# A planned five-engine program: other durations in the table that lays down each engine's order, and another place for two powers of the keys

## The reference, cut to what matters

```python
x = x + tanh(g_xattn[0]) * mamba(ctx, layernorm(x))          # in_proj, conv4, silu, x_proj, softplus,
                                                              # scan over 512 positions for 512 channels x 16 states
x = x + tanh(g_ffn[0])   * out(silu(gate(n)) * val(n))        # n = layernorm(x); three BitLinear layers,
                                                              # weights rounded to -1, 0, 1, rows to 8 bits
x = x + tanh(g_xattn[1]) * (softmax(q_n k_n^T) v) @ Wo        # 16 heads of 128, q and k RMS-normalised, k and v from ctx
x = x + tanh(g_ffn[1])   * down(silu(gate) * up)              # four experts; row r goes to expert r % 4
```

## Time and profile before

| | us |
|---|---|
| three runs | 1846.49, 1849.45, 1853.75 (median 1849.45) |
| the profiled execution | 1849.74, its span 1847.9 |
| PE busy in the span | 1755.0 (95%) |
| DVE, ACT, POOL busy | 1301.5, 963.8, 681.7 |

### The profile page before, as it was taken

The page is one execution under the profiler, slowest core; times in us unless marked ns, Lnnn a source line. Parts: engine busy times, 40 slices in busy tenths (PEclk is TensorE's granted clock), DMA queues, the critical chain, the costliest instruction groups (busy, mean ns, idle before and its releaser), DMA issues.

```text
span 1847.9 us, 19510 instructions
## 1 busy us (share of the span) xinstructions
PE 1755.0 (95%) x6114; PEld 805.4 (44%) x6114; DVE 1301.5 (70%) x1899; ACT 963.8 (52%) x1919; POOL 681.7 (37%) x696
## 2 busy tenths in 40 slices
PE   8999899869998998999999999999999899999999
PEld 4333344324443444444444444444444344445543
DVE  4989786989999699899889898877532444412221
ACT  7989876447555546557466557554444334320100
POOL 2434422356463246457214456642123333300000
PEclk9999999989999999999999999999999999999999
DMA  7999823678851138887115779621122899837110
GB/s 262 244 293 291 259 100 109 188 186 198 207 145 37 52 82 210 222 208 196 57 36 114 178 188 249 159 58 57 46 69 80 235 285 292 237 100 273 40 51 28
DMA packets 159045, 292.11 MB, mean 158 GB/s; under 512 B 18424, under 2 KB 51704, under 8 KB 156000
## 3 DMA queue, kind: packets, MB, share of 16 engines
q1 hardware_dynamic: 141664, 227.95, 39.3%
q0 software_dynamic: 17280, 62.92, 17.6%
HBM read 169.51 MB, written 58.26 MB: 123 GB/s over the span
## 4 chain that ended last, share of the span: by engine, by line
PE 67%; DVE 15%; issue 6%; ACT 5%; DMA 5%; POOL 2%; SPq 1%; DVEq 0%; ACTq 0%; POOLq 0%
PE p L837 10%; PE p L814 8%; PE p L797 8%; PE p L848 7%; PE p L884 6%; PE p L692 5%; DVE s_M L1016 5%; PE p L771 4%; PE p L820 3%; PE p L899 3%; PE p L776 3%; PE p L741 2%; DVE s_M L1011 2%; DVE s_M L1023 2%; DVE s_U L1165 1%
## 5 line engine op out<-in xcount | busy, mean ns | idle before, releaser
L1016 DVE TENSOR_TENSOR_SCAN s_M<-s_M 128x1024 f32<-128x1024 f32 x128 | 297.3, 2323 | 12.5 <-ACT s_M L1277 10.0
L1165 DVE CUSTOM_DVE_ANT_0 s_U<-p,s_U 128x512 f32<-128x512 f32 x256 | 187.7, 745 | 167.0 <-PE p L814 164.7
L814 PE MATMUL p<-s_U 128*128 128x512 f32 x512 | 266.8, 609 | 4.5 <-DVE s_U L1165 3.4
L797 PE MATMUL p<-s_U 128*128 128x512 f32 x512 | 253.6, 604 | 5.1 <-DMA s_U<-in_Wq 2.4
L1517 POOL DMA_DIRECT2D s_u<-s_M x120 | 112.8, 941 | 358.1 <-DVE s_M L1023 323.7
L1558 POOL TENSOR_SCALAR s_U<-s_U 128x512 f32<-128x512 f32 x256 | 237.7, 947 | 6.4
L848 PE MATMUL p<-s_U 128*128 128x512 f32 x512 | 223.7, 592 | 0.0
L837 PE MATMUL p<-s_U 128*128 128x512 f32 x472 | 215.0, 596 | 2.7 <-ACT s_U L1414 2.5
L1414 ACT COPY s_U<-p 128x512 f32<-128x512 f32 x196 | 105.5, 593 | 171.1 <-PE p L820 169.7
L1277 ACT ACTIVATE s_M<-s_dl,s_small 128x511 f32<-128x511 f32 x256 | 170.3, 717 | 45.5 <-DVE s_M L1016 41.8
L1409 ACT ACTIVATE s_U<-s_U 128x512 f32<-128x512 f32 x256 | 181.6, 710 | 5.3
(11 more groups left out here) (194 smaller groups left out, 2469.5 us busy)
## 6 DMA issues: line engine op xcount, KB each, us to landing
s_u<-s_M POOLq DMA_DIRECT2D x120, 512.0 KB, 7.5
s_bc<-bc_scratch SPq DMA_DIRECT2D x96, 256.0 KB, 4.6
k_scratch<-s_U SPq DMA_DIRECT2D x16, 1024.0 KB, 9.0
v_scratch<-s_U SPq DMA_DIRECT2D x16, 1024.0 KB, 6.1
s_U<-in_Wq SPq DMA_DIRECT2D x64, 256.0 KB, 6.6
s_U<-k_scratch SPq DMA_DIRECT2D x64, 256.0 KB, 5.4
s_U<-rk_scratch SPq DMA_DIRECT2D x64, 256.0 KB, 4.8
s_U<-in_Wo SPq DMA_DIRECT2D x64, 256.0 KB, 4.3
```

The lines of the kernel that those rows point to most:

```text
L797: ins = e.matmul(banks[bk][:], wqq[j % 2][:, k, :], axT[b % 2][:, k, :], start=(k == 0), stop=(k == 3))
L814: e.matmul(banks[bk][:], qT[j % 3][:, k * 128:(k + 1) * 128], kT[j % 2], start=True, stop=True).then_inc(S["a_s"], 1)
L1016: e.tensor_tensor_scan(w, dA[i % 2], w, 0.0, ALU.mult, ALU.add).then_inc(S["m_s"], 1)
L1165: e.tensor_tensor_reduce(out=Pm[j % 2][:, k, :], in0=banks[ABANK[kind, j, k]][:], in1=rkb[j % 2], scale=rq[:, k:k + 1], scalar=-3.0e38, op ...
```

## The change

All durations in `mamba`, `forward`, `weights`, `keys` and `context` are written anew, nearly all of them shorter (a decay on ACT 1.43 to 1.24, a score block on DVE 0.85 to 0.78, an exponential of the attention 0.9 to 0.63, a key copy with its square 1.2 to 0.97, a power of the keys stays at 3.0), and the step from one engine to the next counts 0.25 instead of 0.15. Two needs are changed: `pw` of the units (batch 2, q = 3) and (batch 3, q = 3), the last two, now needs `xst 3` of batch 0; and the first scores of head 0 need only the last values of the keys' stream, no longer its last step, the store of the powers. No instruction is added, removed or changed in form, and all semaphore waits stay.

```diff
-            part((kind, i), [("ACT", 1.43)], ("scan", i - (1 if b else 2)) if i >= (1 if b else 2) else ("init", 0))
+            part((kind, i), [("ACT", 1.24)], ("scan", i - (1 if b else 2)) if i >= (1 if b else 2) else ("init", 0))
...
-            part(("xst", t), [("DVE", 1.0), ("POOL", 1.0)], ("l", t, 4))
+            part(("xst", t), [("DVE", 0.83), ("POOL", 0.9)], ("l", t, 4))
...
-        needs = {"nv": [("K", at.get((b, q, "n", 0)))], "n": [("K", at.get((b, q, "k", 3)))], "r": [("K", at.get((b, q, "nv", 0))), ("K", n - 1)], "pw": [("K", at.get((b, q, "r", 0))), ("K", n - 1)], "st": [("K", at.get((b, q, "pw", 0))), ("K", n - 1)]}.get(kind, [])
+        needs = {"nv": [("K", at.get((b, q, "n", 0)))], "n": [("K", at.get((b, q, "k", 3)))], "r": [("K", at.get((b, q, "nv", 0))), ("K", n - 1)], "pw": [("K", at.get((b, q, "r", 0))), ("K", n - 1)] + [(0, "xst", 3)] * (q == 3 and b > 1), "st": [("K", at.get((b, q, "pw", 0))), ("K", n - 1)]}.get(kind, [])
...
-        needs = {"q": [(j // NH, "xxt", 3)] + ([] if j else [("K", KV.index((NB - 1, 3, "n", 0)))]), "nq": [(NB, "q", j, 3)], "nt": [(NB, "nq", j, 0)], "s": [(NB, "nt", j, 0)] + ([] if j else [("K", len(KV) - 1)]) + ([(NB, "t" if on_pe(j - 2) else "tr", j - 2, 3)] if j > 1 else []), "ex": [(NB, "s", j, 3)], "rc": [(NB, "rc", j, k - 1) if k else (NB, "ex", j, 3)],
+        needs = {"q": [(j // NH, "xxt", 3)] + ([] if j else [("K", KV.index((NB - 1, 3, "n", 0)))]), "nq": [(NB, "q", j, 3)], "nt": [(NB, "nq", j, 0)], "s": [(NB, "nt", j, 0)] + ([] if j else [("K", KV.index((NB - 1, 3, "v", 3)))]) + ([(NB, "t" if on_pe(j - 2) else "tr", j - 2, 3)] if j > 1 else []), "ex": [(NB, "s", j, 3)], "rc": [(NB, "rc", j, k - 1) if k else (NB, "ex", j, 3)],
...
-                ready = ended[s, i, k - 1] + 0.15
+                ready = ended[s, i, k - 1] + 0.25
...
-                ready = max([0.0] + [done[n] + 0.15 for n in needs] + [bank[x] for x in take])
+                ready = max([0.0] + [done[n] + 0.25 for n in needs] + [bank[x] for x in take])
```

More of the change, by code:

```diff
@@ L228, in mamba @@
         if kind == "in":
-            part((kind, i), [("PE", 1.75), ("ACT", 1.25)], *([(b - 1, "yt", 3)] if b else []), take=own, free=own)
+            part((kind, i), [("PE", 1.72), ("ACT", 1.2)], *([(b - 1, "yt", 3)] if b else []), take=own, free=own)
         elif kind == "conv":
@@ L232, in mamba @@
         elif kind == "silu":
-            part((kind, i), [("ACT", 3.6 if b else 0.65 if i else 1.9)], ("conv", 3 if b else i))
+            part((kind, i), [("ACT", 3.3 if b else 0.6 if i else 1.85)], ("conv", 3 if b else i))
         elif kind == "xp":
@@ L241, in mamba @@
         elif kind == "dt":
-            part((kind, i), [("PE", 1.0)] + ([("ACT", 0.7)] if b else []), ("xp", 4 if b else 3), take=own, free=own if b else ())
+            part((kind, i), [("PE", 0.9)] + ([("ACT", 0.6)] if b else []), ("xp", 4 if b else 3), take=own, free=own if b else ())
         elif kind == "sp":
@@ L245, in mamba @@
         elif kind == "soft":
-            part((kind, i), [("DVE", 1.25)], ("sp", 0), *([(0, "put", 2, 3)] if b == 1 else []))
+            part((kind, i), [("DVE", 1.15)], ("sp", 0), *([(0, "put", 2, 3)] if b == 1 else []))
         elif kind == "init":
@@ L285, in forward @@
             else:
-                part(name, [("PE", 2.2), ("ACT", 0.7)], ("e", t, 2), *([] if b else [(0, "put", 1, 3)]), take=pair)
+                part(name, [("PE", 2.1), ("ACT", 0.6)], ("e", t, 2), *([] if b else [(0, "put", 1, 3)]), take=pair)
         elif kind == "e":
             if k == 0:
-                part(name, [("DVE", 1.0), ("POOL", 1.1)], ("yt", 3), *([] if b else [(0, "bias", 0, 2)]))
+                part(name, [("DVE", 0.83), ("POOL", 0.9)], ("yt", 3), *([] if b else [(0, "bias", 0, 2)]))
             elif k == 1:
@@ L292, in forward @@
             else:
-                part(name, [("PE", 0.45), ("ACT", 0.7)], ("e", t, 1), take=[("e", t)], free=[("e", t)])
+                part(name, [("PE", 0.4), ("ACT", 0.6)], ("e", t, 1), take=[("e", t)], free=[("e", t)])
         elif kind == "o":
@@ L296, in forward @@
         elif kind == "st":
-            part(("xst", t), [("DVE", 1.0), ("POOL", 1.0)], ("l", t, 4))
+            part(("xst", t), [("DVE", 0.83), ("POOL", 0.9)], ("l", t, 4))
         elif kind == "hn":
-            part(("xhn", t), [("DVE", 0.6)], ("xst", t), ("l", 3, 0))
+            part(("xhn", t), [("DVE", 0.48)], ("xst", t), ("l", 3, 0))
         elif kind == "xt":
-            part(("xxt", t), [("PE", 0.6), ("ACT", 0.7)], ("xhn", t), *([(NB, "q", NH * (b - 1) - 1, 3)] if b > 1 else []), take=[("xt", t)], free=[("xt", t)])
+            part(("xxt", t), [("PE", 0.5), ("ACT", 0.5)], ("xhn", t), *([(NB, "q", NH * (b - 1) - 1, 3)] if b > 1 else []), take=[("xt", t)], free=[("xt", t)])
         elif k == 0:
@@ L305, in forward @@
             pair = [("ht", t, 2 * k - 2), ("ht", t, 2 * k - 1)]
-            part(name, [("PE", 0.6), ("ACT", 1.2)], ("l", t, 0), take=pair, free=pair)
+            part(name, [("PE", 0.55), ("ACT", 0.97)], ("l", t, 0), take=pair, free=pair)
         elif k == 3:
@@ L309, in forward @@
         else:
-            part(name, [("DVE", 0.8)], ("l", t, 3), ("o", t, 0), free=[("o", t)])
+            part(name, [("DVE", 0.67)], ("l", t, 3), ("o", t, 0), free=[("o", t)])
     return out
@@ L318, in weights @@
         if kind == "abs":
-            out.append(("Q", [("DMA", 9.0 if w else (17.0, 4.0, 9.0, 5.0)[c]), ("ACT", 2.0)], [(0, "put", w - 1, c)] if w else [], (0, kind, w, c), [], []))
+            out.append(("Q", [("DMA", 9.0 if w else (17.0, 4.0, 9.0, 5.0)[c]), ("ACT", 1.95)], [(0, "put", w - 1, c)] if w else [], (0, kind, w, c), [], []))
         elif kind == "thr":
@@ L322, in weights @@
         elif kind == "rnd":
-            out.append(("Q", [("ACT", 2.0)], [(0, "thr", w, 0)], (0, kind, w, c), [], []))
+            out.append(("Q", [("ACT", 1.9)], [(0, "thr", w, 0)], (0, kind, w, c), [], []))
         elif kind == "clip":
-            out.append(("Q", [("DVE", 1.3)], [(0, "rnd", w, c)], (0, kind, w, c), [], []))
+            out.append(("Q", [("DVE", 1.15)], [(0, "rnd", w, c)], (0, kind, w, c), [], []))
         elif kind == "put":
-            out.append(("Q", [("ACT", 2.0)], [(0, "clip", w, c)], (0, kind, w, c), [], []))
+            out.append(("Q", [("ACT", 1.82)], [(0, "clip", w, c)], (0, kind, w, c), [], []))
         else:
@@ L338, in keys @@
         bank = KBANK.get(x)
[L339 removed]
+        does = {"k": [("PE", 1.72), ("ACT", 0.97)], "v": [("PE", 1.72), ("ACT", 0.5)], "n": [("PE", 0.9)], "nv": [("ACT", 0.5)],
                 "r": [("DMA", 5.0)], "pw": [("POOL", 3.0)], "st": [("DMA", 8.0 if (b, q) == (NB - 1, 3) else 2.5)]}[kind]
[L341 removed]
+        needs = {"nv": [("K", at.get((b, q, "n", 0)))], "n": [("K", at.get((b, q, "k", 3)))], "r": [("K", at.get((b, q, "nv", 0))), ("K", n - 1)], "pw": [("K", at.get((b, q, "r", 0))), ("K", n - 1)] + [(0, "xst", 3)] * (q == 3 and b > 1), "st": [("K", at.get((b, q, "pw", 0))), ("K", n - 1)]}.get(kind, [])
         take = [bank] if kind in "kvn" else []
```

23 lines of the change are left out of this document (11 added, 12 removed).

## The result

The changed kernel takes 1894.5 us (median of 4 runs, 1884.1 to 1899.6) against 1850.4 before (4 runs); the ratio is 1.023, with a 95% interval of 1.018 to 1.028. Its profiled execution is 1895.8, with a span of 1894.0, 46.1 above that of before. The prediction of 1838.3 was wrong in sign, and the time lies far outside its range.

The account below looks back on a forecast made before the run. PE, busy for 95% of the span, was taken as the bound, so gains must come from its 92.9 us of idle. 1849.74 - 9.4 (transition) - 2.0 (start), middle and end 0, gave 1838.3 us; range 1828 to 1856.

Parts of the forecast that it names:

- The transition, -9.4: 363 to 405 us: DVE's idle of 0.64, 4.52 and 4.24 us goes and comes back as 9.4 us of time.
- The stores and Wo, which give way, are wanted by nothing here: Transition, SP's list: stores of the powers and Wo loads go behind the spreads; stored powers are read from 385; cost nothing.
- Nothing moved lies between these: Transition's end: between DVE's last score block of head 0 and PE's resumption, 4.4 us later, no moved step stands.
- The start, -2, at worst +7: Up to 363 us: small order moves win 2 us; at best -6, at worst two more load waits of 3.5.
- small moves: Start: the order of PE, ACT and DVE is redrawn in moves none of which is over some thirty steps.
- Rival (3): Start: one or two waits of 3.5 us to queued DMAs instead of winning 2; 1844 to 1847 us; chance 0.12.
- The middle, 0, at worst 13.6 for each of two places: 405 to 1400 us: no change; earlier L681 transposes in batches 2 and 3 lose 13.6 each at worst, -6 at best.
- The new numbers are nearer the trace's: Start: durations nearer the trace's let the plan move waits behind other work; at best some third of idle goes, -6.
- rival (2): Start and middle: gaps shrink by 6 and 6 us besides the transition's 9.4, giving 1828.3 us; chance 0.13.
- The rule weighed: Transition: DVE operations with two SBUF inputs and reading POOL operations exclude each other; two powers would hold DVE 8.4 us.
- rival (4): Transition: POOL's two moved powers hold up DVE's multiplications, giving 1846.7 us; chance 0.03.
- POOL is stretched, DVE is not: Near 125 us: a power took 5.17 us while DVE's scan and output beside it kept their usual length.

## Why the prediction was wrong, step by step

**The transition, -9.4.** The mechanism was right and the accounting was not complete. The three waits of DVE went, L749's wait became 7.9 and 6.6 where 6 was forecast, and 7.6 to 8.2 us were won by the first score. The step that failed is "The stores and Wo, which give way, are wanted by nothing here". Nothing wants them, but the load of Wq stands behind them on SP, before and after, and when the rest came 8 us earlier it did not. "Nothing moved lies between these" (score and resumption of PE) failed by the same load: PE waited 3.3 and 2.95 us for it. With it ahead of Wo, 7 us of gain were measured. ("Half of all that is lost per microsecond" is misleading: PE is idle for half of this stage, but the stage holds 21.6 of the 92.9 us.)

**The start, -2, at worst +7: measured +16.8.** The failed step is "small moves" with two waits of 3.5 as the bound. The order was read for PE, ACT and DVE, and SP's for the weights' loads. POOL's list was not read there, nor was SP's store followed to what it waits for. Three accumulations more ahead of one power are 18.8 us here (151.80 to 170.59), and the load behind the store on SP hands them to PE as a wait of 16.2. Rival (3), waits for loads in a full DMA stretch, had the right sign and a small part of the cause: of the two waits for Wk it fits the one of 8.2 us (5.1 before) and not the one of 16.2. The prediction also read the slices of the earlier trace rows wrongly: the full ones are the second to the fourth (46 to 185 us), while the sixth and seventh, which it names, stand at 2 and 3 tenths. That the table kept 5.0 us for the folding DMAs was not what decided: the run with the keys' numbers put back kept it too.

**The middle, 0, at worst 13.6 for each of two places: measured +32.4.** The one place that was costed, L681 in batches 2 and 3, waited 3.5 us in all. The forecast that other steps on DVE move up too was right. What failed is that this place was taken for the whole middle. The heads between (3 to 6, 19 to 25) were not compared, although DVE was busy for 311 of 345 us there, and each of their moves is repeated in every head: 3.9 us in a plain head. The term that the sum lacked is the scan ahead of four scores, held by POOL's multiplications for 2.2 us: seven times, with waits of PE of 15.4 us and a lower clock behind six of them (below).

**"The new numbers are nearer the trace's"** stood behind rival (2) and the -2. Three rows of ACT in the changed kernel:

```profile
411.08 0.72 ACT L1409 ACTIVATE s_U<-s_U 128x512 f32<-128x512 f32 x1
411.71 0.19 ACT L1409 ACTIVATION_READ_ACCUMULATOR s_U<-s_U 128x1 f32 x1
411.80 0.70 ACT L1409 ACTIVATE s_U<-s_U 128x512 f32<-128x512 f32 x1
```

The 0.63 is the distance to the accumulator read; one exponential follows another after 0.72 (411.08 to 411.80). The old number of 0.9 was farther from that than the new one, and the order that came out of it was better by 20 us.

**The rule weighed.** DVE ran its steps at their usual length beside POOL's powers of the keys in the transition (2.29 and 1.22 us beside power 15, which took 4.42), so rival (4) did not come where it was expected. But "POOL is stretched, DVE is not" was read from one POOL instruction, the power of the keys. Beside the multiplications L1558 whoever came second waited, as the rule has it, and that was DVE seven times in the middle (4.47 us instead of 2.29). In the kernel before it was POOL: its longest multiplication beside a scan took 2.8 us, the median of all is 0.7. The prediction priced the rule at the two powers of the transition alone.

**The end, 0:** +1.7, within what single executions differ by.

## What to carry over

In a planned program, a table's numbers are inputs of an order and not measurements: numbers closer to the trace can give a worse order, so compare the lists of all engines before and after, the helper queues first, and in a repeated stretch compare one whole period. When a step is moved behind another on a queue, ask not only who wants the moved step but who stands behind it. A stall that one engine's list shows may move on when that list is mended; put the input back before you name the row as the cause. And when an instruction runs longer than others of its kind, it is not waiting in its list: look at what the other engines do beside it.
